# Causal attention in a two-layer block: the order of the 16 transfers of a group of probabilities

## The reference

```
qkv = einsum('bse,ehd->bshd', x, qkv_w) + qkv_b
q, k, v = split(qkv, 3, axis=-1)
logits = einsum('bqhd,bkhd->bhqk', q, k) / sqrt(64)
logits = where(tril, logits, very_negative)
probs  = softmax(logits, axis=-1)
attn   = einsum('bhqk,bkhd->bqhd', probs, v)
out    = einsum('bqhd,hde->bqe', attn, out_w) + out_b
```

## Time and profile before

| | us |
|---|---|
| median of 3 runs | 1485.28 |
| lowest and highest | 1480.12, 1485.90 |
| profiled execution | 1482.89 |
| its span, first to last instruction | 1481.2 |

### The profile page before, as it was taken

The page is one execution under the profiler, slowest core; times in us unless marked ns, Lnnn a source line. Parts: engine busy times, 40 slices in busy tenths (PEclk is TensorE's granted clock), DMA queues, the critical chain, the costliest instruction groups (busy, mean ns, idle before and its releaser), DMA issues.

```text
span 1481.2 us, 27229 instructions
## 1 busy us (share of the span) xinstructions
PE 1417.2 (96%) x9282; PEld 914.2 (62%) x9282; DVE 1255.7 (85%) x1966; ACT 916.9 (62%) x1862; POOL 968.5 (65%) x756
## 2 busy tenths in 40 slices
PE   8989999999999999999999998889999999999998
PEld 6755556555555565565655555456667676776767
DVE  7587888788877888888888777479999999999997
ACT  3456666666666667666666675557665675657562
POOL 5144555546555456455555554549999999999895
PEclk9999999999999999999999999999999999999999
DMA  8059777877787778777777778400000000000000
GB/s 189 1 129 217 173 172 179 185 170 175 174 185 173 172 173 186 172 168 178 181 181 166 178 177 199 102 1 1 0 9 8 1 8 1 8 8 1 8 1 15
DMA packets 77140, 163.98 MB, mean 111 GB/s; under 512 B 31410, under 2 KB 43724, under 8 KB 77004
## 3 DMA queue, kind: packets, MB, share of 16 engines
q1 hardware_dynamic: 77004, 162.24, 47.5%
HBM read 9.08 MB, written 2.10 MB: 8 GB/s over the span
## 4 chain that ended last, share of the span: by engine, by line
PE 81%; DVE 7%; issue 5%; POOL 3%; ACT 2%; SPq 0%; DMA 0%; DVEq 0%; ACTq 0%; POOLq 0%
PE accum L1095 17%; PE both L1030 12%; PE misc L997 9%; PE both L2785 8%; PE flips_all L1030 5%; PE flips_all L2808 4%; PE flips_all L1119 4%; PE misc L1007 4%; PE flips_all L2797 3%; PE flips_all L2845 2%; PE accum L2797 2%; PE accum L2808 2%; ACT big L533 2%; PE flips_all L2831 1%; PE flips_all L968 1%
## 5 line engine op out<-in xcount | busy, mean ns | idle before, releaser
L452 POOL TENSOR_SCALAR big<-big,recip 128x384 f32<-128x384 f32 (+7 forms) x512 | 374.4, 745 | 430.5 <-DVE recip L704 430.5
L712 DVE STREAM_TRANSPOSE big<-big 128x896 f32<-128x896 f32 (+7 forms) x288 | 346.0, 1227 | 17.5 <-POOL big L452 16.8
L533 ACT ACTIVATE big<-both,neg_max 128x1024 f32<-128x1024 f32 (+3 forms) x256 | 243.1, 955 | 162.7 <-DVE neg_max L694 157.5
L1095 PE MATMUL accum<-across,v_sb 128*64 128x256 f32 (+1 forms) x2560 | 272.8, 364 | 22.2 <-issue 21.8
L1095 PEld LDWEIGHTS accum<-across,v_sb 128*64 128x64 f32 x2560 | 187.0, 138 | 137.9 <-issue 82.5
L694 DVE TENSOR_REDUCE neg_max<-both 128x1 f32<-128x1024 f32 (+3 forms) x256 | 248.3, 1011 | 7.6 <-PE both L1035 7.6
L1030 PE MATMUL both<-qk_sb 64*128 64x512 f32 (+3 forms) x1024 | 212.9, 532 | 13.1 <-issue 8.2
L533 ACT ACTIVATE big<-flips_all,neg_max 128x128 f32<-128x128 f32 (+3 forms) x256 | 131.6, 525 | 102.7 <-DMA across<-big 59.8
L2785 PE MATMUL both<-slow_sb,h_T 128*128 128x512 f32 x384 | 181.2, 599 | 7.9 <-DVE xnT L2298 4.4
L1594 POOL TENSOR_TENSOR prod<-xnT,qs 128x1024 f32<-128x1024 f32 (+3 forms) x32 | 180.2, 5638 | 11.1 <-DVE qs L2298 11.1
L1030 PEld LDWEIGHTS both<-qk_sb 64*128 64x128 f32 x1024 | 94.1, 186 | 117.9 <-issue 117.9
(11 more groups left out here) (224 smaller groups left out, 2404.9 us busy)
## 6 DMA issues: line engine op xcount, KB each, us to landing
across<-big SPq DMA_DIRECT2D x1024, 144.0 KB, 3.1
out<-x SPq DMA_DIRECT2D x8, 256.0 KB, 2.3
x<-in_L_attn_x SPq DMA_DIRECT2D x3, 512.0 KB, 5.5
slow_sb<-in_L_attn_w_slow SPq DMA_DIRECT2D x3, 512.0 KB, 7.1
w_qk<-in_L_attn_qkv_w SPq DMA_DIRECT2D x2, 512.0 KB, 6.3
xn<-in_L_ffn_W SPq DMA_DIRECT2D x1, 1024.0 KB
x<-in_L_attn_x SPq DMA_DIRECT2D x2, 256.0 KB, 3.0
qs<-in_L_attn_qkv_w SPq DMA_DIRECT2D x1, 512.0 KB, 6.0
```

The source lines that it names most:

```text
L452: pool.tensor_scalar(part, part, recip[:, u % 2, SLOTS.index(row), h:h + 1], 0.0, ALU.mult, ALU.add).then_inc(scaled, 1)
L533: last = act.activation(probs_of(row, h).rearrange("p b j k -> p j b k"), scores_of(row, h).rearrange("p (j b k) -> p j b k", b=MOVES, k=3 ...
L712: dve.transpose(part, part).then_inc(turned[group_of(row)], 1)
L1095: last = pe.matmul(dst, lhsT=values_of(u, j, h), rhs=keys_of(g, rows[n:n + 2], j, h), start=j == 0, stop=j == rows[n + 1])
```

## The change

Only the loop that issues a burst is changed. The pairs of source quarter a and destination quarter b are the same 16; their order is another.

```
-                for a in range(MOVES):
-                    for b in range(MOVES):
+                for k in range(MOVES):
+                    for a in (0, 2, 1, 3):
+                        b = a ^ k
                         sp.dma_start(across[g][32 * b:32 * (b + 1), a, :], runs[g][32 * a:32 * (a + 1), b, :]).then_inc(moved[g], 16)
```

## The result

| | before | after |
|---|---|---|
| median, us (4 runs each) | 1483.10 | 1468.59 |
| lowest to highest, us | 1480.12 to 1485.90 | 1461.97 to 1469.89 |
| profiled execution, us | 1482.89 | 1468.25 |
| its span, us | 1481.2 | 1466.5 |

The ratio is 0.9894, with a 95% interval of 0.9872 to 0.9916 (the quotient of the two medians alone is 0.9902). The change made the kernel about 1% faster, 14.5 us by the medians and 14.6 us by the profiled executions. Forecast were 1470 us, from a term of 15.3 us against the median of the first three runs before, 1485.28.

The account below looks back on a forecast made before the run. PE was taken to bound the kernel, standing in a loop for group 1's last landing. Terms of 13.7 + 0.8 + 0.8 = 15.3 us against the median of 1485.28 gave 1470 us, range 1463 to 1485.

Parts of the forecast that it names:

- The loop: Group 1 in attention: a period is the burst with its landing plus 13.7 us from PE's restart to the next burst.
- step 3: PE's 27 waits ahead of x40 blocks: each gives the smaller of its wait and 0.8 us, 13.7 us in all.
- step 5: End of attention, unit 30: PE's 4.23 us wait for group 1 shortens by 0.8 us; clock change costed at nothing.
- Step 1: Landing of a burst's transfers: with neighbours reading different halves no queue builds, 0.8 us off each burst.
- Step 2: SP's issues within a burst: they stay 0.64 us apart, as before.
- rival (c): Issues in a burst: stepping halves on both sides makes each longer, 20 us slower, 1505 us; chance 5%.
- rival (b): Bursts: the queue goes, but SP's stops and late transfers come through in full; 8 us gained, 1477 us; chance 20%.
- The floor: Period in attention once PE itself is late: 12.6 + 13.7 = 26.35 us, so 28 periods give at most 18 us.
- Step 4: Group 0's bursts: no gain, as PE is busy until they land, except 0.8 us in unit 0.
- Rival (a): Bursts: transfers are served one after the other, so no relief; 1485 us, within 0.5%; chance 17%.

Follow-up runs that it names:

- e3: Against the kernel before, the source quarter changes at every transfer, but its half only after eight and the destination's half after every four: 1494.90 us, ratio 1.0075.
- e1: Against the kernel before, the source alternates halves at every transfer while the destination stays in one half for eight: 1498.55 us, ratio 1.0101.
- e5: Against the kernel before, only group 0's bursts take the new order, group 1's keep the old one: 1481.34 us, ratio 0.9988.
- e2: Against the kernel before, the destination alternates halves at every transfer while the source stays in one half for eight: 1478.64 us, ratio 0.9965.
- e10: The changed kernel with one of group 1's sixteen transfers issued by ACT, ahead of row 7's exponentials: 1464.81 us, ratio 0.9874 to the kernel before.
- e11: The changed kernel with ACT issuing two of group 1's transfers apart, ahead of row 7's and row 6's exponentials: 1464.16 us, ratio 0.9869 to the kernel before.
- e7: The changed kernel with ACT issuing two of group 1's sixteen transfers, both ahead of row 7's exponentials: 1478.45 us, ratio 0.9954 to the kernel before.

## Why the prediction was right

The loop, its fixed part and the size of the relief were right. The reason for the relief was half of the truth, and the sum came as near as it did partly by luck. Of the 14.7 us between the two profiles, 12.5 us belong to step 3 (13.7 forecast: 1.3 + 11.6 less the 0.4 of unit 0), 0.6 us to step 5 (0.8 forecast), none to unit 0 (0.8 forecast), 1.2 us to a clock that the sum held at nothing, and 0.54 us, less 0.15 us lost again in unit 0, to the time ahead of the first burst. Without these two some 13 us of the 15.3 came.

**Step 1, the landing: right in size, incomplete in its reason.** 0.8 us were taken off, 0.7 to 0.8 us went. The prediction read the rate jump of the earlier trace rows as the state with both halves in flight and held that the half is what counts, which e3 confirms for reading. But it held that "the destination cannot explain the jump" and argued by reads alone. The destination matters as much: e1, with perfect alternation of the source, is the slowest kernel of all. The change worked because it alternates both sides; reads alone would have made 1% slower what was forecast 1% faster. That the order chosen moved the destination too was, by the argument given, luck. The prediction's words "the destination also changes half at each step" hold for 14 of the 15 steps (not from 32 to 02). The arithmetic of the queue was also off: 0.06 us more for each transfer would add up evenly over the burst, but before the landings rise by 0.77 us up to the eighth transfer (2.40 to 3.17, some 0.11 for each) and by 0.08 us in the eight after it. The rates of the earlier trace rows could hardly have told this. Two stretches of the burst of e1, from 2 us after its first issue on, and below them the first such stretch of after (busy us of the engines, then granted clock, DMA share, GB/s):

```profile
536.60:541.60 5.00, 4.73 (x36) 2.43 (x31) 3.04 (x7) 3.98 (x14) 2.71 (x4) 1.00 0.99 231
541.60:546.60 5.00, 5.00 (x32) 2.54 (x32) 5.00 (x10) 3.55 (x7) 2.44 (x5) 1.00 1.03 210
...
523.00:528.00 5.00, 4.73 (x34) 2.43 (x30) 3.04 (x7) 3.98 (x14) 2.75 (x4) 1.00 1.00 238
```

In the first half of e1's burst the landings have grown from 2.5 to 3.3 us while the rate, 231 GB/s, is near the 238 of after, where none grows; only in the second half does it fall, to 210. The landings tell it sooner. Where between the read and the landing that queue stands no record shows.

**Step 2, issues: right.** The median issue stayed at 591 to 592 ns in after; rival (c) is out.

**Step 3, how much PE can use: a little too high.** Forecast were 13.7 us over the units with a wait, measured 12.5 us, as said. In after 10 waits are left ahead of an x40 block, 0.10 to 1.05 us and 4.5 us in sum, where 16.3 us had been. Six of them stand behind bursts in which single issues of SP took 1.0 to 2.0 us, and four behind a last landing of 3.1 to 4.1 us, whose cause no run shows. That is rival (b): the queue had hidden part of such a stop, and now it comes through. It was real, but took 1.2 us of the 13.7 and not 6. The floor held: the undisturbed period from 507.26 to 533.63 is 26.37 us against a forecast of 26.35.

**Step 4, group 0: right** for the loop, within what e5 can tell. The one exception in it failed: unit 0's wait was said to shorten by 0.8 us and is 1.57 us instead of 1.42. It ends 0.4 us earlier (97.32 against 97.71), but PE and the burst had started 0.54 us earlier. The landing did improve, by 1.0 us: the last transfer came 97.62 - 94.10 = 3.5 us after its issue before and 97.23 - 94.74 = 2.5 us in after. What took it back are SP's stops. The burst of before and that of after (issues in ns, first and last start in us):

```profile
L354 SPq DMA_DIRECT2D across<-big x16: 590/595/1447, 84.5 to 94.1; - x16
...
L355 SPq DMA_DIRECT2D across<-big x16: 590/592/1840, 83.9 to 94.7; - x16
```

The longest issue was 1.84 us instead of 1.45, and the 15 gaps made 10.8 us instead of 9.6. This is rival (b) again, in one place at full size. And in unit 30 of after PE stands for group 0 where it did not before, behind a burst with a landing of 4.5 us. It cost nothing: the burst of group 1, which sets PE's next stop, had started before that wait ended (894.18 us) and as early as elsewhere, 12.8 us ahead of before (907.02).

```profile
893.14 1.67 issue
```

**Step 5, the end: nearly right.** The wait went from 4.23 to 3.34 us, 0.9 us for the 0.8. At the start of the block it is 0.6 us: PE came to the wait 12.6 us earlier than before, after 12.9 us at the block of unit 29. The last landing was late in both kernels, 4.7 us after its issue before and 4.0 in after, for a cause that no run shows. The clock fell here again, but for a shorter part of the block. These stretches of after answer to the earlier trace rows (busy us of the engines, then granted clock, DMA share, GB/s): 3.4 us at 0.50 instead of 6.8, worth 1.2 us of the 2.9 kept for the range. It goes with the shorter wait in the other profiles too: the clock was low for 6.8 us behind the waits of 4.9 us in e1 and 5.5 us in e3, and for 3.4 us behind that of 2.8 us in e2.

```profile
904.60:907.90 3.30, 0.02 (x1) 0.00 (x0) 2.77 (x4) 0.00 (x0) 1.09 (x2) 1.00 0.39 99
908.70:912.10 3.40, 3.40 (x22) 2.51 (x20) 2.77 (x4) 2.31 (x6) 1.15 (x2) 0.50 0.64 146
```

**Rival (a), no relief: out.** The Trainium skill, page "SBUF — State Buffer", section "Can I just issue two DMAs to hit both halves?", answers no: two concurrent DMAs, at partitions 0 and 64, measured 6% over one. No run here shows such a pair. Taken strictly for this stream of transfers it was rival (a), and the landings rule that out. The gain was also more than its 6%: by the estimate that the prediction made from it, 0.02 us of queue for each transfer would be left, and the sixteenth lands no later than the first (2.44 and 2.42 us). The supply of 230 GB/s is 9% above the 211 GB/s of one half, and it was met.

## What to carry to other kernels

When many small transfers between quarters of the partitions are issued in a row, let every neighbour pair differ in the half (0 to 63, 64 to 127) on the source side and on the destination side; one side alone can be worse than neither. What this is worth is read at the last landing of a burst and at who waits for it: here 0.75 us per burst in a loop where the next burst could only start a fixed 13.7 us after the landing, until PE itself took over, 0.6 us of a period further on. If the issue then sets the pace, a second issuer can help where its issue ends inside a wait that it has anyway; here it removed PE's waits (e10, e11), and where it ended later it cost 9 us (e7).

## What the runs showed that was not expected

- Both sides of a half queue. Eight transfers in a row out of one half (e2) or into one half (e1) bring the eighth landing to 3.15 and 3.22 us, from 2.4 and 2.5. The second eight, on the other half, add nothing when they read from it (3.11 us at the sixteenth) and 0.4 us when they write to it (3.65 us).
- The queue of e1 shows in the time from issue to landing before it shows in the rate of the transfers.
- Two issues back to back on ACT, beside a busy SP, took 1.90 us together (e7), while single ones took 0.51 to 0.52 us (e11). Whether ACT's second issue waits for its own first or for SP's was not tried.
